# The first expert pair's w1 products for four batches inside the second pass of a fused Mamba and soft-MoE block, B and C merged, and a new order of visits

## The reference

```python
h = _layernorm(x) * (1 + ca) + sa
x = x + ga * _L0_attn_ref(h, ...)
h = _layernorm(x) * (1 + cb) + sb
x = x + gb * _L0_ffn_ref(h, ...)

# mixer, on xn = rmsnorm(h): z, x_ssm, Bm, Cm, dt_raw = slices of xn @ in_proj_w.T
x_conv = silu(conv_b + sum over 4 taps of shifted x_ssm * conv_w)
h = h * dA_t + dtx_t * B_t          # for each of 4 heads, over the tokens
y_t = einsum('bhpn,bhn->bhp', h, C_t)
y = (y + D * xh) * silu(z)
out = h_in + y @ out_proj_w.T

# experts: 8 of them, 64 slots each
logits = einsum('bnd,esd->bnes', xn, sn)
dispatch, combine = softmax over tokens, softmax over all slots
slots = einsum('bnd,bnes->besd', xn, dispatch)
h = gelu(einsum('besd,edh->besh', slots, w1) + b1)       # hidden size 512
eo = einsum('besh,ehd->besd', h, w2) + b2
out = einsum('bmd,bnm->bnd', eo, combine)
```

## Time and profile before

| | us |
|---|---|
| median of 3 runs | 230.07 |
| lowest, highest | 229.61, 230.66 |
| the profiled execution's own time | 228.26 |
| its span | 226.3 |
| granted TensorE clock | 1.00 |

### The profile page before, as it was taken

One profiled execution on the slowest core, in us unless ns is written; L12 is line 12 of the kernel. 1 busy time (PEld: TensorE's weight loads), 2 busy tenths in 40 slices (PEclk: granted clock), 3 DMA queues, 4 the chain that ended last, 5 costly groups with the idle time before them and its releaser, 6 DMA issues.

```text
span 226.3 us, 4248 instructions
## 1 busy us (share of the span) xinstructions
PE 206.5 (91%) x1575; PEld 149.1 (66%) x1575; DVE 137.8 (61%) x372; ACT 120.1 (53%) x264; POOL 59.9 (26%) x147
## 2 busy tenths in 40 slices
PE   3779999996799999999996799989999999999993
PEld 2546476674477795565674486774956849569993
DVE  3698859998999857859998865530220402204662
ACT  3688996532479756895523576658145081450000
POOL 6553884026524203983025500000000000000000
PEclk9999999999999999999999999999999999999999
DMA  6404002000500000002400000014133041300122
GB/s 192 116 0 141 6 5 75 20 3 16 202 15 3 0 3 0 1 2 66 125 0 1 0 3 0 3 52 133 49 93 96 1 138 49 93 3 3 58 70 61
DMA packets 15345, 10.73 MB, mean 47 GB/s; under 512 B 1773, under 2 KB 13654, under 8 KB 15326
## 3 DMA queue, kind: packets, MB, share of 16 engines
q1 hardware_dynamic: 15100, 10.31, 15.2%
q10 hardware_dynamic: 226, 0.16, 0.3%
HBM read 9.34 MB, written 1.07 MB: 46 GB/s over the span
## 4 chain that ended last, share of the span: by engine, by line
PE 63%; DVE 20%; ACT 6%; issue 4%; POOL 2%; DMA 2%; ACTq 1%; DVEq 0%; POOLq 0%
PE bank L577 28%; PE bank L922 13%; PE bank L904 11%; DVE seg_m L1370 5%; PE bank L814 2%; DVE bst L1183 2%; DVE hh L1246 2%; DVE cshift L1407 2%; DMA vec_nat<-ffn_slot_norm_gamma_dram 2%; PE bank L829 2%; DVE hh L1238 2%; DVE x1tok L1388 1%; DVE xhT L1379 1%; PE bank L761 1%; PE bank L835 1%
## 5 line engine op out<-in xcount | busy, mean ns | idle before, releaser
L1444 DVE TENSOR_TENSOR eo<-bank,seg_e 128x512 f32<-128x512 f32 x8 | 5.5, 692 | 47.9 <-PE bank L922 47.9
L922 PEld LDWEIGHTS bank<-w_sb,zsT 128*64 128x64 f32 x256 | 27.8, 137 | 3.0 <-issue 3.0
L922 PE MATMUL bank<-w_sb,xcT 128*64 128x128 f32 x256 | 28.8, 273 | 0.0
L922 PE MATMUL bank<-w_sb,zsT 128*64 128x128 f32 x256 | 28.8, 273 | 0.0
L922 PEld LDWEIGHTS bank<-w_sb,xcT 128*64 128x64 f32 x256 | 27.8, 137 | 0.0
L904 PE MATMUL bank<-slotsT,w_sb 128*128 128x512 f32 (+1 forms) x64 | 26.1, 558 | 0.2 <-ACT zsT L1140 0.2
L1140 ACT ACTIVATE zsT<-bank,vecT 128x512 f32<-128x512 f32 x16 | 10.7, 687 | 24.9 <-PE bank L904 24.9
L577 PE MATMUL bank<-xnT,winT 128*128 128x512 f32 x48 | 22.4, 603 | 0.0
L490 POOL TENSOR_TENSOR root<-root,neg_half 128x2 f32<-128x2 f32 (+1 forms) x24 | 20.2, 843 | 2.0
L1306 DVE SCALAR_TENSOR_TENSOR xcT<-bank,convw,xcT 128x510 f32<-128x510 f32 (+2 forms) x24 | 17.3, 736 | 4.5 <-ACT xcT L1050 4.2
L904 PEld LDWEIGHTS bank<-slotsT,w_sb 128*128 128x128 f32 x64 | 11.4, 190 | 12.6 <-issue 12.1
(11 more groups left out here) (165 smaller groups left out, 412.9 us busy)
## 6 DMA issues: line engine op xcount, KB each, us to landing
w_sb<-in_L_ffn_w_dram SPq DMA_DIRECT2D x16, 256.0 KB, 2.8
mods_bc<-mod_dram SPq DMA_DIRECT2D x4, 320.0 KB, 3.4
xin<-in_L_attn_x_dram SPq DMA_DIRECT2D x4, 256.0 KB, 2.8
out_dram<-x1tok SPq DMA_DIRECT2D x16, 64.0 KB, 1.5
mods_bc<-mod_dram SPq DMA_DIRECT2D x4, 192.0 KB, 3.1
seg_e<-mod_dram SPq DMA_DIRECT2D x1, 512.0 KB, 3.9
eo<-in_L_attn_in_proj_w_dram SPq DMA_DIRECT2D x1, 384.0 KB, 3.9
eo<-in_L_wmod_dram SPq DMA_DIRECT2D x1, 256.0 KB, 4.4
```

The source lines that it names most:

```text
L922: q = nc.tensor.matmul(o[j * S:(j + 1) * S, tile_cols(b)], act_h[j][k // 2][:, k % 2, at:at + S], w2_sb[j][:, k, :], start=k == 0 and b == ...
L1444: V.tensor_tensor(o, bank[4 + 2 * (it % 2) + g][:, :].rearrange("p (b d) -> p b d", d=P), b2_bc[:, it, :].unsqueeze(1).broadcast_to((P, 4, ...
```

## The change

1. **B and C merged.** B and C are used in scores alone, as C_t . B_s = xn_t . (Wc' Wb) . xn_s. The product of the two weight blocks is made once (128 columns, in place of two transposes), and project1 makes `UT` from it where it made B. scores reads `UT` against `xnT`. The product for C and ScalarE's copy of C go, four times each. `winT` is 128 columns narrower; `xn2T` has a tensor of its own.
2. **Products ahead.** In the second pass first_hidden multiplies w1 of experts 0 and 1 with the slots of batches 0 to 3 (256 columns a product): four products behind y_of of half 0, for two of the four blocks of the hidden size, into half 0's banks 2 and 3, and four more in half 1's. copy_hidden (ScalarE) copies each bank into rows of `act_h`, dead by then. logits waits for it. Behind the last visit first_gelus applies the gelu to those rows in place (8 of 256 columns). early_hidden and hidden(0) do batches 4 and 5, then 6 and 7, of both experts (128 columns a product, 16 products), both experts in one bank, and gelus(0) are 8 of 256 columns. outputs(0) waits for first_gelus in `g` = 0 and for gelus(0) in `g` = 1.
3. **Visits split.** scores, copy_scores, t_xh, dt_times_x, add_basis (now gated_h and add_x), gate_weights, first_tap and norm_slots go by batch or block; t_logits by token tile; y_of gives its products with D to d_times_x and waits for each pair of heads; shifts and the exps are two visits each; the centring of the second norm is centre2; fill_slots orders its eight products so that the second token tile's exps are awaited later.
4. **New turns** in every table, and the loads of w1 are issued in the first pass.

```diff
...
-    Z0, X0, B0, C0 = 0, DI, 2 * DI, 2 * DI + P
+    Z0, X0, U0, DTC = 0, DI, 2 * DI, 2 * DI + P
+    B_BLOCK, C_BLOCK = 2 * DI // P, 2 * DI // P + 1
...
-            for n in range(ROW_BLOCKS):
-                q = nc.tensor.transpose(bank[1 + n // 4][:, tile_cols(n % 4)], w_nat[:, n, :], ident[:, :])
+            for n in range(2 * CT):
+                nc.tensor.transpose(bank[1][:, tile_cols(n)], w_nat[:, n, :], ident[:, :])
+            mm(bank[2][:, 0:P], w_nat[:, B_BLOCK, :], w_nat[:, C_BLOCK, :])
...
-                mm(b2[:, :], winT[:, B0:B0 + P], xnT[j][:, :]).then_inc(proj_ps[1][j], 1)
+                mm(b2[:, :], winT[:, U0:U0 + P], xnT[j][:, :]).then_inc(proj_ps[1][j], 1)
...
-                mm(bank[4 * j + 3][:, :], winT[:, C0:C0 + P], xnT[j][:, :]).then_inc(proj_ps[1][j], 1)
...
-                    mm(o[:, 0:L], BT[j][:, t0:t0 + P], CTr[j][:, t0:t0 + L])
-                    mm(o[:, L:L + P], BT[j][:, t0 + P:t0 + L], CTr[j][:, t0 + P:t0 + L]).then_inc(g_ps[1][j], 1)
+                    mm(o[:, 0:L], UT[j][:, t0:t0 + P], xnT[j][:, t0:t0 + L])
+                    mm(o[:, L:L + P], UT[j][:, t0 + P:t0 + L], xnT[j][:, t0 + P:t0 + L]).then_inc(g_ps[1][j], 1)
...
+                            if g == 0 and h % 2 == 0:
+                                wait(pe, m_done, j, it, 3 * bi + h // 2 + 1)
+                            elif h == 0:
+                                wait(pe, m_done, j, it, 3 * bi + 3)
...
+            def first_hidden(j, it):
+                if it < PASSES - 1:
+                    return
+                wait(pe, seg_done, j, it)
+                for i in range(2):
+                    wait(pe, slotsT_done, i, 0)
+                for e in range(2):
+                    wait(pe, w1_in, e, 0)
+                    for i in range(2):
+                        q = nc.tensor.matmul(bank[4 * j + 2 + e][:, i * AHEAD * S:(i + 1) * AHEAD * S],
+                                             w1_sb[e][:, tile_cols(2 * j + i)],
+                                             slotsT[:, e, 0:AHEAD, :].rearrange("p b s -> p (b s)"),
+                                             start=i == 0, stop=i == 1, skip_group_check=True)
+                    q.then_inc(ahead_ps[j], 1)
...
+                        if it == PASSES - 1:
+                            pe.wait_ge(ahead_done[j], 2)
...
+            def last_hidden(k, e, b0, b1):
+                at = ((b0 - AHEAD) + (1 - e) * AHEAD) * S
+                return nc.tensor.matmul(bank[k][:, at:at + (b1 - b0) * S], w1_sb[e][:, tile_cols(k)],
+                                        slotsT[:, e, b0:b1, :].rearrange("p b s -> p (b s)"),
+                                        start=b0 == AHEAD and e == 0, stop=b1 == B, skip_group_check=True)
             def early_hidden():
                 wait(pe, slotsT_done, 0, PASSES - 1)
-                wait(pe, slotsT_done, 1, 0)
-                wait(pe, w1_in, 0, 0)
                 for k in range(HC):
-                    nc.tensor.matmul(bank[k][:, 0:EARLY * S], w1_sb[0][:, tile_cols(k)],
-                                     slotsT[:, 0, 0:EARLY, :].rearrange("p b s -> p (b s)"),
-                                     start=True, stop=False, skip_group_check=True)
+                    for e in range(2):
+                        last_hidden(k, e, AHEAD, EARLY)
...
+                if it == 0:
+                    for k in range(HC):
+                        for e in range(2):
+                            last_hidden(k, e, EARLY, B).then_inc(hid_ps[1][e], 1)
+                    return
...
+                        if g == 0 and it == 0:
+                            pe.wait_ge(gelu_ahead, 2 * (k + 1))
+                        for j in range(2):
+                            if g == 0:
                                 wait(pe, w2_in, j, it)
+                            if g == (it == 0):
                                 wait(pe, gelu_done, j, it, k + 1)
...
+            def copy_u(j, it):
                 wait(act, proj_ps, j, it, 4)
-                A(BT[j][:, :], bank[4 * j + 2][:, :], ACT.Copy).then_inc(xbc_done[1][j], 1)
+                A(UT[j][:, :], bank[4 * j + 2][:, :], ACT.Identity, scale=vecT[:, RNW:RNW + 1]).then_inc(xbu_done[1][j], 1)
...
-            def copy_c(j, it):
-                wait(act, proj_ps, j, it, 5)
-                A(CTr[j][:, :], bank[4 * j + 3][:, :], ACT.Copy).then_inc(xbc_done[1][j], 1)
...
+            def copy_hidden(j, it):
+                if it < PASSES - 1:
+                    return
+                for e in range(2):
+                    act.wait_ge(ahead_ps[j], e + 1)
+                    if e == 0:
+                        wait(act, yg_done, j, it)
+                    else:
+                        wait(act, y_ps, j, it)
+                    A(act_h[e][j][:, :, 0:AHEAD * S], bank[4 * j + 2 + e][:, :].rearrange("p (i c) -> p i c", i=2), ACT.Copy
+                      ).then_inc(ahead_done[j], 1)
+            def first_gelus():
+                for k in range(HC):
+                    act.wait_ge(ahead_done[k // 2], 2)
+                    for e in range(2):
+                        h = act_h[e][k // 2][:, k % 2, 0:AHEAD * S]
+                        A(h, h, ACT.Gelu, bias=vecT[:, RB1 + e * HC + k:RB1 + e * HC + k + 1]).then_inc(gelu_ahead, 1)
...
+                if it == 0:
+                    for k in range(HC):
+                        for e in range(2):
+                            wait(act, hid_ps, e, it, k + 1)
+                        for e in range(2):
+                            at = (1 - e) * AHEAD * S
+                            A(act_h[e][k // 2][:, k % 2, AHEAD * S:], bank[k][:, at:at + AHEAD * S], ACT.Gelu,
+                              bias=vecT[:, RB1 + e * HC + k:RB1 + e * HC + k + 1]).then_inc(gelu_done[1][e], 1)
+                    return
...
+                      ((44, 48, 122, 126), project_out(1)), ((45, 52, 125, 128), first_hidden),
...
+                      ((45, 47, 109, 113), mean_squares2(0)), ((46, 52, 110, 114), copy_hidden),
...
+            pipeline(sp, [((5, 7, 3, 8), next_x), ((6, 9, 11, 10), next_mods), ((0, 4, 12, 13), send_parts)], once=[(2, lambda: load_w1(0, 0)), (1, lambda: load_w1(1, 0))])
```

309 lines of the change are left out of this document (166 added, 143 removed).

## The result

The changed kernel took **220.08 us** (median of four runs, 218.62 to 221.77) against 229.97 for the kernel before beside it: ratio 0.957, 95% interval 0.949 to 0.965. A second set gave 220.23 and 0.960 (0.953 to 0.967). A median is over all executions of a set, a ratio over the faster ones alone, against the kernel before beside them, so that the two need not agree. Predicted were 221.9 and a range of 219.2 to 226.2. The profiled execution took 219.09 us with a span of 217.0, against 228.26 and 226.3.

The account below looks back on a forecast made before the run. Bounds: TensorE and ScalarE at each pass's head, TensorE waiting for VectorE at the mixer's end, TensorE in the tail. 0.6 + 3.2 + 0.8 - 0.9 + 4.5 = 8.2 us off 230.07 gives 221.9, range 219.2 to 226.2.

Parts of the forecast that it names:

- Head, 0.6: Before pass 0's projections: VectorE makes the unit tokens first, taking 0.6 us off the chain TensorE's transposes wait for.
- B and C merged, 3.2: Projections of both passes: four 512-column products and ScalarE's copies go, saving 3.2 us between bounds of 2.0 and 3.5.
- Leaves GpSimd's queue of such work where it is, so I take nothing for it: GpSimd's addition of x beside VectorE's casts: halved but not moved, counted as 0, at most 0.6 us a pass.
- the dangers: Half 1 held back by the new TensorE order and GpSimd's gate products behind all additions: kernel slower, chance 0.05.
- End of the mixer, 0.8: Centring behind half 1's gate(1) and y_of's finer waits: 0.8 us in the first pass, the second counted with products ahead.
- Products ahead, -0.9: Second pass: 3.5 us of w1 products fill TensorE's 3.4 us of waits; copies and squares ahead of copy_xn2T make it cost 0.9.
- The rival that the work isn't hidden: Second pass grows by 4.5 us instead of 0.9 through the products ahead, giving 225.5 us; chance 0.14.
- Start of the tail, 4.5: From the last slot product to the first w2 product: 4.6 us instead of 9.1, a gain of 4.5.
- the gelus at 0.40: ScalarE at the start of the tail: gelus of 256 columns take 0.4 us each, so the w2 products never wait.
- the signs named: w2 after 4.6 us, project_out directly behind first_hidden, the 1.19 wait gone, first pass 2.8 shorter, 67.8 us from w2 to end.
- rival two: ScalarE sets the projections: merging brings 2.0 us instead of 3.2 and the gate orders nothing, giving 223.9 us; chance 0.10.
- The rival that GpSimd's halved additions block VectorE for shorter times: VectorE's casts beside GpSimd's additions of x: 0.6 us more saved in each pass, giving 220.7 us; chance 0.03.

Follow-up runs that it names:

- before_merged_centre: The kernel before with B and C merged and centre2 in the changed kernel's places, nothing else: 226.32 us, ratio 0.994.
- c_product: The changed kernel with C's 512-column product put back in each half's projections, without ScalarE's copy: 221.89 us, ratio 0.975.
- pool_wait: The changed kernel with GpSimd, after softplus of half 1, also waiting until VectorE has made that half's three parts: 221.26 us, ratio 0.965.
- no_ahead: The changed kernel without first_hidden, copy_hidden and first_gelus, the first expert pair done as in the kernel before: 222.86 us, ratio 0.973.

## Why the prediction was right

220.08 lies in the range, just under the forecast's own width (from 220.5), and the sum of 8.2 meets 8.35 in the stages. The medians differ by more, 9.9 us: 1.0 is the last write, and the other 0.5 stays open; it is less than executions of one kernel differ by. The sum's terms were not all right: errors cancelled. Right by mechanism is the start of the tail; that the head and the passes met their sum is luck.

- **Head, 0.6.** Not to be told: project1 starts at 15.55 before and at 15.14 after, but at 15.04 in before_merged_centre, which lacks the new turn, and at 15.84 in c_product, which has it.
- **B and C merged, 3.2.** The step that failed is to price a product by its length and to take it off a stage without a hole. Alone it brings 0.04 in the second pass. In the new order TensorE sets the stage, and there the product's price is 1.45 in the second pass and 1.39 in the first, by TensorE's share and not ScalarE's; that GpSimd's new turn is what made the difference is read from rows. "Leaves GpSimd's queue of such work where it is, so I take nothing for it" was wrong: gate_weights moved behind softplus of half 1, which the order of GpSimd's instructions showed, and I had this turn among the dangers and not among the gains.
- **End of the mixer, 0.8.** 0.5 in the first pass and 0.85 in the second when done in the kernel before; 0.9 and 1.5 when undone. Mis-sized, and I had counted the second pass as the room for the work ahead.
- **Products ahead, -0.9.** It is -0.15. I counted the holes of before (3.4) right, and then added 0.8 for the copies ahead of copy_xn2T. In the trace after copy_xn2T's result is waited for 0.53 us, and without the copies 0.50: they stand in ScalarE's idle time (the first begins at 117.32, behind 3.93 us without work). The rival that the work isn't hidden falls.
- **Start of the tail, 4.5.** 9.1 became 4.7: right, and so were the gelus at 0.40. Of the 4.85 us from the shifts to the w2 product 3.78 are the work ahead's, 1.07 those of the split norm_slots and of t_slots moved up.

Together head and passes were to give 3.7 and gave 3.5: merging and centring by themselves 1.3, the start 0.4, the work ahead -0.15, and 1.9 are left for the rest of the new order in the passes. No run tells these 1.9 apart, and they belong to the order with the two edits in it: undone, the product for C costs 2.8 and the turn of centre2 2.4. Of the signs named, all but the last came: w2 after 4.7 us, project_out directly behind first_hidden, the wait of 1.19 gone, a first pass shorter by 2.7 at its shifts (2.8 named). From the first w2 product to the end it is 66.9 instead of 67.8, by the last write alone. ScalarE as the bound of the projections (rival two) is excluded by c_product, which pays 2.8 without any copy. The rival that GpSimd's halved additions block VectorE for shorter times falls: in the changed kernel's first pass its last three operations on the parts of half 1 take 0.75, 0.65 and 0.64 us, and TensorE waits 1.24 for them in the second.

## What to carry to other kernels

What an edit is worth depends on which engine is late when it comes: price it by doing it alone and by undoing it in the finished kernel, and look at the queue of the least busy engine (GpSimd was busy for 26%), since by the rows its order decided whether 3 us of TensorE work counted. Compare executions at the same granted clock: for pool_wait and no_ahead the medians alone told the price wrong by 1 us or more. Work of a later stage that fits the length of the holes of an earlier one was nearly free here (0.15 us for 3.5), copies included, since the copying engine idles there too. And where operands lie in SBUF, moving GpSimd's work changed whom it slows, in both runs that moved it, and not whether.
